# First layer's splat products as 64-column diagonal tiles, x's load ahead of the masks, output stored by blocks in a two-layer kernel

## The reference, cut to what matters

```python
xn = _layernorm(x, axis=-1)
# first attention, 16 heads of 16 dims, 8 splats per head
diff = x[:, :, :, None, :] - splat_positions[None, :, None, :, :]
gauss = jnp.exp(-0.5 * jnp.sum(diff * diff, -1) / (scales ** 2)[None, :, None, :])
dirp = jnp.tanh(jnp.einsum('bhsnd,hnd->bhsn', diff, dirn))
# end of the second layer
out = h + moe(rmsnorm(h, ln2_w), ...)      # 8 experts: 1 shared, 7 routed
x = x + _L1_attn_ref(xn, ...) + out
```

## Time and profile before

| | |
|---|---|
| runs | 1911.91, 1907.4, 1913.23 us; median 1911.91 |
| profiled execution | 1912.08 us |
| its span on the chip | 1910.4 us |
| mean granted TensorE clock | 0.926 of full speed |
| busy: PE, DVE, ACT, POOL | 88%, 77%, 65%, 37% of the span |
| masks end, x's first load issued | 6.8 us |
| splat stage | about 54 to 134.7 us |
| its last store issued | 144.4 us |
| last DVE operation, end of span | 1903.1 us, 1910.4 us |

### The profile page before, as it was taken

The page is one execution under the profiler, slowest core; times in us unless marked ns, Lnnn a source line. Parts: engine busy times, 40 slices in busy tenths (PEclk is TensorE's granted clock), DMA queues, the critical chain, the costliest instruction groups (busy, mean ns, idle before and its releaser), DMA issues. The chain is left out here.

```text
span 1910.4 us, 31941 instructions
## 1 busy us (share of the span) xinstructions
PE 1689.1 (88%) x10554; PEld 1172.0 (61%) x10554; DVE 1467.5 (77%) x3080; ACT 1234.5 (65%) x2769; POOL 697.7 (37%) x1326
## 2 busy tenths in 40 slices
PE   4979899999999878788889998888876899987998
PEld 3547644444444467667668876776754545545887
DVE  6767689999998267999997869999446788916654
ACT  2534377887778533789886768888752688865222
POOL 2002212222222214666665646666232111125532
PEclk9989899999999899888889999889987799987999
DMA  3364122233320200000000000000037222110001
GB/s 121 116 215 89 34 54 55 62 68 68 68 60 10 75 1 1 1 1 1 1 1 1 1 1 1 1 1 1 1 115 186 43 56 56 35 74 1 1 1 45
DMA packets 36132, 82.27 MB, mean 43 GB/s; under 512 B 9856, under 2 KB 11776, under 8 KB 34944
## 3 DMA queue, kind: packets, MB, share of 16 engines
q1 hardware_dynamic: 35968, 80.22, 16.8%
HBM read 52.53 MB, written 27.26 MB: 42 GB/s over the span
## 5 line engine op out<-in xcount | busy, mean ns | idle before, releaser
L1140 ACT ACTIVATE probs<-pss 128x512 f32<-128x512 f32 (+3 forms) x1152 | 481.8, 496 | 129.0 <-PE pss L1103 127.9
L848 DVE TENSOR_REDUCE negmax<-px 128x2 f32<-128x1024 f32 (+2 forms) x480 | 508.5, 1113 | 45.5 <-PE px L830 42.6
L1697 POOL TENSOR_SCALAR rp<-sw,tau 128x256 f32<-128x256 f32 x720 | 341.8, 507 | 7.1
L1207 POOL TENSOR_SCALAR_AFFINE_SELECT probs<-probs 128x512 f32<-128x512 f32 x192 | 120.4, 635 | 506.8 <-ACT probs L1140 506.8
L1103 PE MATMUL pss<-queries,keys 64*128 64x512 f32 (+3 forms) x1152 | 295.9, 396 | 5.5 <-ACT probs L1140 4.3
L830 PE MATMUL px<-keys,queries 63*128 63x512 f32 (+3 forms) x1152 | 266.8, 420 | 10.5 <-DVE negmax L848 10.5
L1103 PEld LDWEIGHTS pss<-queries,keys 64*128 64x128 f32 x1152 | 167.6, 190 | 152.3 <-ACT probs L1140 134.5
L1117 PE MATMUL po<-probs,vals 128*32 128x512 f32 (+3 forms) x2304 | 248.7, 508 | 0.4 <-POOL probs L1207 0.2
L1546 PE MATMUL pss<-again,sw 128*128 128x256 f32 x1024 | 247.0, 400 | 0.0
L1851 DVE BATCH_NORM_STATS2 st<-rp 128x6 f32<-128x512 f32 x360 | 229.7, 675 | 2.3 <-POOL rp L1697 2.3
L1546 PEld LDWEIGHTS pss<-again,sw 128*128 128x128 f32 x1024 | 205.5, 205 | 29.3
(11 more groups left out here) (375 smaller groups left out, 2587.1 us busy)
## 6 DMA issues: line engine op xcount, KB each, us to landing
queries<-rec_q SPq DMA_DIRECT2D x96, 128.0 KB, 3.4
keys<-rec_k SPq DMA_DIRECT2D x96, 128.0 KB, 3.5
queries<-rec_q SPq DMA_DIRECT2D x96, 64.0 KB, 3.4
keys<-rec_k SPq DMA_DIRECT2D x96, 64.0 KB, 3.4
rec_q<-fs SPq DMA_DIRECT2D x16, 256.0 KB, 4.4
rec_k<-fs SPq DMA_DIRECT2D x16, 256.0 KB, 4.9
rec_q<-vals SPq DMA_DIRECT2D x16, 256.0 KB, 3.1
rec_k<-vals SPq DMA_DIRECT2D x16, 256.0 KB, 3.6
```

The lines of the kernel that those rows point to most:

```text
L848: return e.tensor_reduce(out, from_px, X_AXIS, ALU.max, negate=True)
L1140: e.activation(tl.probs[arg][:, w, :], tl.pss[scores % 3][:, 512 - width:512], ACT.Exp).then_inc(self.exp_made, 1)
L1697: x = e.tensor_scalar(self.rp[rp % 6][:, :, h], self.view(g, q)[:, h, :], -BIG, self.tau[r][:, 2 * q + h:2 * q + h + 1], ALU.min, ALU.max)
```

## The change

- The constants that `FirstNorm` needs (`ident`, `eps`) and the masks become two classes. `Constants`, `FirstNorm` and `Masks` are put together into one stage with `Together`, which calls the parts' methods one after the other on each engine. SP has nothing ahead of x's load any more; POOL makes `ident` and `eps`, then clears `vals`, then makes the masks. PE and ACT of `FirstNorm` wait for the two constants.
- The six splat products of a round are each made with 64 of the 128 weight columns, into 64 of the 128 PSUM partitions: chunk 0 with columns and partitions 0 to 63, chunk 1 with 64 to 127. The 64 columns left out of each hold zeros. Columns streamed (512) and the number of instructions stay.
- The stage `Store` goes. SP of `OutputAndExperts` waits on `y_read` and stores blocks 0 to 2 (512 KB each) as they become final, and the four 128-token tiles of block 3 (128 KB each) one by one.

```diff
@@ Constants / Masks
+class Constants(Stage):
+    def __init__(self, k):
+        self.k = k
+        k.ident, k.eps = k.sb("ident", [P, P]), k.sb("eps", [P, 1])
+        self.cleared, self.made = k.sems("cleared made")
+    def pool(self, e):
+        k = self.k
+        e.memset(k.ident[:], 0.0).then_inc(self.cleared, 1)
+        e.wait_ge(self.cleared, 1)
+        e.affine_select(out=k.ident[:], in_=k.ident[:], compare_op=ALU.not_equal, fill=1.0, base=0, pattern=[[-1, P]],
+                        channel_multiplier=1).then_inc(self.made, 1)
+        e.memset(k.eps[:], EPS).then_inc(self.made, 1)
...
@@ FirstNorm.pe, FirstNorm.act
+        e.wait_ge(self.constants.made, 2)
...
@@ QueriesAndKeys.pe
-            products(e, self.gp[s][:], [(self.half[:, c, :], self.sq[s][c][:]) for c in range(DC)]
-                     + [(self.pos[:, c, :], self.raw[s][c][:]) for c in range(DC)]).then_inc(self.gauss_in, 1)
+            for first, weights, of in ((True, self.half, self.sq), (False, self.pos, self.raw)):
+                for c, at in self.halves():
+                    x = e.matmul(self.gp[s][at, :], weights[:, c, at], of[s][c][:], start=first, stop=not first,
+                                 skip_group_check=True)
+            x.then_inc(self.gauss_in, 1)
...
-            products(e, self.dp[s][:], [(self.dirs[:, c, :], self.raw[s][c][:]) for c in range(DC)]).then_inc(self.dir_in, 1)
+            for c, at in self.halves():
+                x = e.matmul(self.dp[s][at, :], self.dirs[:, c, at], self.raw[s][c][:], start=True, stop=True)
+            x.then_inc(self.dir_in, 1)
+    def halves(self):
+        return [(c, slice(c * HALF, (c + 1) * HALF)) for c in range(DC)]
...
@@ OutputAndExperts.sp
+        for i in range(NB - 1):
+            e.wait_ge(self.y_read, 4 * NE * (i + 1))
+            e.dma_start(k.out[:, 4 * i:4 * i + 4], k.x[:, 4 * i:4 * i + 4]).then_inc(self.stored, 16)
+        for t in range(4):
+            e.wait_ge(self.y_read, 4 * (NB * NE - 1) + t + 1)
+            e.dma_start(k.out[:, NT - 4 + t], k.x[:, NT - 4 + t]).then_inc(self.stored, 16)
+        e.wait_ge(self.stored, 16 * (NB + 3))
...
-class Store(Stage):
-    def sp(self, e):
-        e.dma_start(self.k.out, self.k.x[:]).then_inc(self.stored, 16)
-        e.wait_ge(self.stored, 16)
...
@@ stages
-                        out += [FirstNorm(k, rest, weights), rest]
+                        out += [Together(constants, FirstNorm(k, constants, rest, weights), masks), rest]
...
```

More of the change, by code:

```diff
@@ L147, in __init__ @@
         self.k = k
-        k.ident = k.sb("ident", [P, P])
+        k.ident, k.eps = k.sb("ident", [P, P]), k.sb("eps", [P, 1])
[7 more added lines that the diff above has]
+        e.memset(k.eps[:], EPS).then_inc(self.made, 1)
+class Masks(Stage):
+    def __init__(self, k):
+        self.k = k
         k.mask_of = k.sb("mask_of", [P, 2, P], BF16)
         k.mask_by = k.sb("mask_by", [P, 2, 2, HALF], BF16)
-        k.eps = k.sb("eps", [P, 1])
-        self.made = k.sem("constants")
+        self.made = k.sem("made")
     def pool(self, e):
         k, step = self.k, Steps(self.made)
-        for t in (k.ident, k.mask_of):
-            step(e.memset(t[:], 0.0))
+        step(e.memset(k.mask_of[:], 0.0))
         step(e.memset(k.mask_by[:], BIG))
-        step(e.memset(k.eps[:], EPS))
         e.wait_ge(self.made, step.n)
@@ L165, in keep @@
             e.wait_ge(self.made, step.n)
-        keep(k.ident[:], ALU.not_equal, 0, [[-1, P]], 1, 1.0)
         for half in (0, HALF):
@@ L214, with __init__ @@
 class FirstNorm(Stage):
-    def __init__(self, k, rest, rounding):
-        self.k, self.rest, self.rounding = k, rest, rounding
+    def __init__(self, k, constants, rest, rounding):
+        self.k, self.constants, self.rest, self.rounding = k, constants, rest, rounding
         self.vals, self.xh, self.xl = k.vals, k.xh, k.xl
@@ L2307, in __init__ @@
          self.lo_made, self.steps, self.sig_made, self.gate_in, self.up_in, self.silu_made, self.fused, self.h_added,
-         self.y_in, self.y_read, self.dh_made, self.dl_made, self.zh_made, self.zl_made, self.shared) = k.sems(
+         self.y_in, self.y_read, self.dh_made, self.dl_made, self.zh_made, self.zl_made, self.shared,
+         self.stored) = k.sems(
             "wo_loaded small_loaded loaded dw_loaded o_made o_turned ot_made o_in added stats var_made squares root_made "
             "rms_made xn_made turned xh_made xl_made xs_made logits_in logits_out hi_made lo_made steps sig_made gate_in "
-            "up_in silu_made fused h_added y_in y_read dh_made dl_made zh_made zl_made shared")
+            "up_in silu_made fused h_added y_in y_read dh_made dl_made zh_made zl_made shared stored")
     def sp(self, e):
@@ L2607, in pool @@
             e.sem_clear(sem)
-class Store(Stage):
-    def __init__(self, k):
-        self.k, self.stored = k, k.sem("stored")
-    def sp(self, e):
-        e.dma_start(self.k.out, self.k.x[:]).then_inc(self.stored, 16)
-        e.wait_ge(self.stored, 16)
 def stages(k):
@@ L2629, in stages @@
     k.hop_mean, k.hop_scale, k.rms = k.sb("hop_mean", [P, NT]), k.sb("hop_scale", [P, NT]), k.sb("rms", [P, NT])
-    out = [Constants(k)]
+    constants, masks, out = Constants(k), Masks(k), []
     with ExitStack() as kept:
@@ L2668, in stages @@
         out.append(OutputAndExperts(k))
-    return out + [Store(k)]
+    return out
 def two_layer_kernel(nc, ins, out):
```

## The result

| | before | after |
|---|---|---|
| median of the runs | 1912.57 us (1907.4 to 1915.73, 6 runs) | 1899.12 us (1897.49 to 1900.94, 6 runs) |
| ratio | | 0.9942, 95% interval 0.9928 to 0.9955 |
| profiled execution, its span | 1912.08 us, 1910.4 us | 1899.34 us, 1897.6 us |
| mean granted TensorE clock | 0.926 | 0.927 |
| x's load issued; statistics start | 6.88; 14.25 us | 0.80; 8.22 us |

The changed kernel is faster by 0.58%, which by the interval of the ratio is 8.6 to 13.8 us. The span fell by 12.8 us, which divides as follows, each term a difference between two landmarks of the table, before less after: 4.8 us up to the first `dims` (56.94 - 52.11), 4.4 us from there to DVE's last work of the stage (77.72 - 73.28), -0.6 us from there to the last accumulation (1768.44 - 1769.00), and 4.1 us behind it.

The account below looks back on a forecast made before the run. PE works nearly throughout, but the edits touch the opening's serial waits, the feature stores pacing the splat stage at 9.5 us a round, and the final store. Gains 5.5 + 2.0 + 4.1 = 11.6 us gave 1900.3 us, range 1895.5 to 1906.

Parts of the forecast that it names:

- The forecast's own case: Whole kernel: all three edits gain and feature stores pace the splat stage; 11.6 us gained, 1900.3 us, chance 78%.
- The load ahead of the masks: Opening: x's first load goes out 6.05 us earlier; gain 5.5 us, bounds 3.25 and 6.05.
- The contention: Opening: DVE's seven small operations run beside POOL's last selects; cost taken as 0.55 us, at most 2.8.
- The rule about the port: Opening: two-input DVE instructions and GpSimd SBUF reads exclude each other; by it alone, gain near the lower bound.
- The splat products: Splat stage: paired 64-column products start the chain of stores earlier; gain 2.0 us at stage's end, bounds nothing and 4.0.
- from there the chain runs at 9.5 us a round as now: Splat stage, after round 1's stores: the pace of stores stays 9.5 us a round, so the 2.0 us reach the end.
- PE as the bound: Splat stage: PE sets the pace and its whole 20.6 us saving reaches the end; 1881.7 us, chance 3%.
- Tiles that don't overlap: Splat stage: 64-column products are as slow as before and give nothing; 1902.3 us, chance 10%.
- lose the clock: Splat stage: products neither overlap nor keep PE's clock, which stays at its lower level; 1948.8 us, chance 3%.
- Two gains staying away: Whole kernel: two of three gains fail, say slow small operations and a 6.3 us last store; 1906.3 us, chance 6%.
- The output by blocks: Kernel's end: early block stores save the barrier and most of the transfer; gain 4.1 us, bounds 3.6 and 4.65.
- SP needs 0.34 per issue: Kernel's end: earlier 128 KB stores don't hold up the last, issued at about 1903.2 just after the last accumulation.

Follow-up runs that it names:

- the start alone: Kernel before with only the split constants and masks and the earlier load of x; splat products at full width, one final store: 1904.95 us, ratio 0.9974.
- stores ahead: Changed kernel with the next round's `dims` records stored ahead of each round's features: 1899.86 us, ratio 0.9948 to the kernel before.
- the store alone: Kernel before with only the output stored by blocks: 1905.5 us, ratio 0.998.

## Why the prediction was right

The forecast was 1900.3 us and the result 1899.12; measured again it was 1902.53. The gain forecast was 11.6 us; by the ratios it was 11.1 us (8.6 to 13.8) and then 7.8 us (5.3 to 10.5). So the size is right within the scatter, and that the first result lies only 1.2 us from the forecast is in part luck. The forecast's own case came true where the runs can tell: the gains at the start and at the end of the kernel are there with their mechanisms, the stores bound the splat stage, and no rival's mechanism appeared. That the tiles' 2 us arrive at the end isn't shown.

- **The load ahead of the masks: 5.5 forecast, 4.8 to 5.0 measured.** The load's step was right (0.80 us, statistics at 8.22, masks done at 14.22 where I had worked out about 14.5). Two errors in the rest stand against each other. The contention that I priced at 0.55 us, between bounds of 0 and 2.8, was 0.08: 1.16 us for the seven operations instead of 1.08 (1.08 to 1.20 in the ten profiles with this start). And a cost had no term in the sum: the table load behind the variance, 1.1 us, which the run with the waits swapped gives back. I read the added wait as one that is long fulfilled, which it is, and didn't ask which instruction carries which wait. The order of the instructions with their waits shows it before any run.
- **The rule about the port.** The Trainium skill ("SBUF — State Buffer", on the shared port pair) has two-input operations of DVE and SBUF reads of GpSimd exclude each other. By it alone the gain would have been near the lower bound, 3.25. The trace doesn't agree here: seven operations, five of them started beside the selects, took 0.08 us more in all, and the five last selects took 2.34 us before and after, though beside POOL's subtractions such operations had taken three times as long. Why selects disturb so much less than subtractions no run here shows.
- **The splat products: 2.0 forecast, 4.4 read in the profile, of which 1.9 can be put down to the tiles.** "A pair should take about one product's 0.86 us" became 0.91 and 0.86. The first feature stores moved by 1.65 us against the stage's first splat product, where I had 1.75, and the gap in front of round 1's stores, for which I had 0.2, closed by 0.3 in this profile. The other 2.5 us of the profile aren't from the tiles. 0.96 us is the stretch from the first `dims` to the first splat product (8.28 to 7.32 us), which depends on how long PE's clock is at its lower level there: in before from the first `dims` to 62.6 us (56.94 to 62.6, products 0.43 us apart), in after only from 53.6 to 57.2 us, with the other products 0.23 apart. The stretch is 8.3 to 8.5 us in three profiles (before, the start alone, stores ahead) and 7.1 to 7.3 in the others of the table, with tiles and without (7.22 in the store alone). Some 1.5 us are the rate at which the stores land, which moves by as much from run to run. The tiles' ratio alone, 0.9996, fits 2 us of gain (0.9990) and fits none, and at the stage's end the means with and without tiles are 0.6 us apart inside the scatter. The step from the first store to the stage's end ("from there the chain runs at 9.5 us a round as now") is thus neither confirmed nor refuted: the rounds take 9.1 to 9.5 us at full width and 9.35 to 9.8 with tiles.
- **PE as the bound** (second rival): excluded by PE's wait of 20.54 us for DVE and by the two runs without feature stores, between which the tiles are worth 8.9 us.
- **Tiles that don't overlap, or lose the clock** (first and last rival): excluded by pairs of 0.86 to 0.91 us and PE's round in 5.71 us against the 5.4 that I gave. A round's three pairs take 2.73 us, 0.15 above three times 0.86. The first rival's time, 1902.3, can't be told from the forecast by the runs; it is its mechanism that is excluded.
- **Two gains staying away** (third rival): excluded by the small operations' 0.08 us and a last store that lands in 1.9 us.
- **The output by blocks: 4.1 forecast, 4.09 in the profile**, 3.8 by the ratio of the store alone. The sum is right and its terms are off in opposite ways: the last store lands 1.9 us after its issue instead of 2.6, and goes out 0.8 us behind the last accumulation instead of 0.1. "SP needs 0.34 per issue" was the part that failed: the four issues take 0.33 to 0.69 us each and do hold one another up. The landing is nearer to the small transfer of 2.04 us than to the 256 KB store, which I had preferred as going to DRAM too.

The sum was 11.6 us. What the profiles attribute to the edits for certain is 4.8 + 4.1 = 8.9 us, and at most the tiles' 1.9 beside it, 10.8; the rest of the first profile's 12.8 us is scatter in its favour, and the second measurement's 7.3 us (1909.85 less 1902.53) has it the other way.

## What to carry to other kernels

An engine that works without a gap isn't the bound if the next stage's first product waits for another engine: halving the time of its splat products here moved the first store by 1.65 us and the stage's end by no more than the runs can tell, and taking the true limit away made the same edit worth 8.9 us. Where a limit is the landing of stores, look for every wait that hangs on them, since putting one out of the way (order of the queue, two sets of tiles) leads to the next, and a new buffer's own release is one more. And when a wait is added in front of an activation that needs a new table, write the wait that is fulfilled last nearest to the activation only after reading which instruction will carry it: here the wait written last went to the table load.

## What the runs showed of the hardware that I had not expected

- The load of ACT's table is an instruction of its own with a place of its own among the waits. Of two waits ahead of the activation, the table load took the one written last and the activation the other; exchanging them brought `pt` from 17.30 to 16.21 us, and before, with the one wait, the table load ran at 16.83 us, 3.86 us ahead of the variance.
- Selects on POOL, beside which five of DVE's seven small operations start, cost 0.08 us over the seven, and none to 0.12 us in the ten profiles with this start.
- The same 1.77 ms of products take 1765 to 1773 us, the shorter times at the higher granted clock (0.933 to 0.917). An edit worth 2 us can't be seen in the time beside it, and can in a distance between two landmarks that doesn't contain it (9.95 us four times in the table, 8.30 or 8.31 seven times).
- The queue moves a round of eight 256 KB stores in 9.1 to 9.8 us in the seven profiles with SP's first order of stores, with no gain from a faster PE: 9.12, 9.48 and 9.48 at full width, 9.35 to 9.79 with tiles.
